# Delta-rule chunk tables: two stages of 256 tokens each against one stage of four units of 128 tokens

## The reference, cut to what matters

```
def step(S, inp):
    qt, kt, vt, at, bt = inp
    v_hat = einsum('bij,bi->bj', S, kt)
    err = vt - v_hat
    S = at * S + bt * (kt[:, :, None] * err[:, None, :])
    o = einsum('bij,bi->bj', S, qt)
    return (S, o)
_, O = lax.scan(step, S0, (Q, Kh, V, alpha, beta))
```

## Time and profile before

| | |
|---|---|
| time, median of 3 runs | 5346.77 us (5340.24 to 5348.16) |
| profiled execution, time | 5344.06 us |
| profiled execution, span | 5342.3 us |
| DVE busy | 4191.0 us (78%) |
| PE busy | 3706.5 us (69%) |
| ACT busy | 3022.2 us (57%) |
| POOL busy | 2649.8 us (50%) |

### The profile page before, as it was taken

How to read it: one execution, slowest core, us unless ns; L and a number is a source line. 1 busy time by engine, 2 the same in 40 slices (tenths; PEclk the granted TensorE clock), 3 DMA queues, 4 the chain that set the end, 5 groups by cost and what they waited for, 6 DMA issues and landing times. The chain is left out here.

```text
span 5342.3 us, 68134 instructions
## 1 busy us (share of the span) xinstructions
PE 3706.5 (69%) x15374; PEld 1423.1 (27%) x15374; DVE 4191.0 (78%) x7837; ACT 3022.2 (57%) x4244; POOL 2649.8 (50%) x2095
## 2 busy tenths in 40 slices
PE   7983000222222279698859999999999999999569
PEld 3431000122122234233213333333333333333123
DVE  5544956999999765426879999999999999999352
ACT  5575000222222155433728989898989898999432
POOL 1000644888888510120735666666666666666312
PEclk9997555666666699899979999999999999999789
DMA  1017054343344300001441111111111111110300
GB/s 43 8 42 125 8 91 88 80 88 85 77 87 88 85 25 10 10 0 74 159 137 34 35 35 34 34 35 35 35 31 33 25 34 35 35 35 5 103 10 32
DMA packets 143839, 275.50 MB, mean 52 GB/s; under 512 B 73808, under 2 KB 87504, under 8 KB 136336
## 3 DMA queue, kind: packets, MB, share of 16 engines
q1 hardware_dynamic: 142128, 263.57, 21.1%
q10 hardware_dynamic: 1440, 8.65, 0.5%
HBM read 178.65 MB, written 93.36 MB: 51 GB/s over the span
## 5 line engine op out<-in xcount | busy, mean ns | idle before, releaser
L1027 POOL TENSOR_TENSOR att_heads_rest<-att_heads_probs,att_heads_high 128x576 f16<-128x576 f32 x1024 | 1393.3, 1361 | 843.6 <-ACT att_heads_high L1114 836.9
L1144 DVE TENSOR_REDUCE att_heads_maxima<-att_heads_peek 128x1 f32<-128x512 f32 x2048 | 1311.3, 680 | 99.2 <-PE att_heads_peek L1040 71.1
L1112 ACT ACTIVATE att_heads_probs<-att_heads_scores 128x1024 f32<-128x1024 f32 x1024 | 1075.3, 1050 | 246.3 <-PE att_heads_scores L1058 237.9
L1058 PE MATMUL att_heads_scores<-att_heads_q,att_heads_k 128*128 128x512 f16 (+1 forms) x4096 | 1068.0, 383 | 34.2 <-issue 21.5
L1114 ACT ACTIVATE att_heads_high<-att_heads_scores 128x1024 f16<-128x1024 f32 x1024 | 1076.4, 1051 | 0.0
L1770 PE MATMUL delta_scan_sums<-delta_scan_o_halves,main_identity 128*128 128x256 f32 x768 | 245.4, 494 | 1111.2 <-POOL delta_scan_o_halves L1845 1111.2
L1164 DVE TENSOR_TENSOR att_heads_rest<-att_heads_probs,att_heads_high 128x448 f16<-128x448 f32 x1024 | 888.5, 868 | 64.8 <-POOL att_heads_rest L1027 53.3
L1040 PE MATMUL att_heads_peek<-att_heads_k,att_heads_q 112*128 112x512 f16 x2048 | 686.2, 396 | 89.1 <-DVE att_heads_maxima L1144 46.4
L1058 PEld LDWEIGHTS att_heads_scores<-att_heads_q,att_heads_k 128*128 128x128 f16 (+1 forms) x4096 | 394.6, 98 | 459.4 <-ACT att_heads_high L1114 39.8
L1770 PEld LDWEIGHTS delta_scan_sums<-delta_scan_o_halves,main_identity 128*128 128x128 f32 x768 | 194.4, 258 | 1162.6 <-POOL delta_scan_o_halves L1845 1124.4
L1074 PE MATMUL att_heads_out<-att_heads_high,att_heads_v_head 128*64 128x512 f16 x2048 | 419.3, 406 | 3.7 <-DVE att_heads_rest L1164 2.9
(11 more groups left out here) (243 smaller groups left out, 5180.4 us busy)
## 6 DMA issues: line engine op xcount, KB each, us to landing
delta_scan_record<-delta_record SPq DMA_DIRECT2D x64, 1026.0 KB, 10.9
att_heads_q<-att_hel SPq DMA_DIRECT2D x192, 128.0 KB, 3.1
att_heads_k<-att_hel SPq DMA_DIRECT2D x192, 128.0 KB, 3.2
delta_record<-delta_chunks_record SPq DMA_DIRECT2D x64, 256.5 KB, 4.8
att_hel<-att_hel_high SPq DMA_DIRECT2D x32, 512.0 KB, 4.4
att_hel<-att_hel_rest SPq DMA_DIRECT2D x32, 512.0 KB, 5.0
att_o<-att_heads_out_copy SPq DMA_DIRECT2D x256, 32.0 KB
att_out_parts<-att_o ACTq DMA_DIRECT2D x8, 1024.0 KB, 13.2
```

Of the source, the lines that this page charges most:

```text
L1027: nc.gpsimd.tensor_tensor(rest[:, step % 4, SPLIT:], probs[:, step % 4, SPLIT:], high[:, step % 4, SPLIT:], ALU.subtract).then_inc(rest_b_ ...
L1058: mm = nc.tensor.matmul(scores[:, step % 2, tokens(j)], k[0:rows, slot, number, tile * P:(tile + 1) * P], q[0:rows, slot, number, tokens(h ...
L1112: nc.scalar.activation(probs[:, step % 4], scores[:, step % 2], ACT.Exp, scale=LOGIT_SCALE).then_inc(probs_ready, 1)
L1144: nc.vector.tensor_reduce(maxima[:, m:m + 1], peek[:, m % 2], AX.X, ALU.max).then_inc(peek_read, 1)
```

## The change

The two calls become one, which goes over four units of 128 tokens of each part (16 chunks, two runs).

- Device memory: `delta_q` and `delta_k` become `(batch, part, unit, channel, 128)`; their stores in `delta_normalise` write pieces of 512 bytes. `delta_v` and the records keep their form.
- SP loads keys and queries of one unit, 8 + 8 transfers of 128 KB, into the single buffer `raw`, in the order (i, t); the load of unit u+1 is issued ahead of the stores of unit u, once both tiles of unit u have been turned. ACT issues the loads of the decays for all 512 tokens.
- ACT copies `raw` into `kq` in the order (t, i) (`turn`, one instruction for keys and one for queries, 2048 elements in a partition each, two buffers) and copies the turned keys into PSUM (`bank`, 2048 elements, one buffer).
- `gram` lies in PSUM. DVE's own products read the keys from PSUM (`k_bank`) and the other operand from SBUF. K_OUT reads `k_bank` too, 16 elements apart, and is made ahead of the solve.
- A row instruction now covers 16 chunks, so it has (t + w) x 256 elements. Of the 15 rows of a unit POOL multiplies 11 (44 x 256 elements in all, three slots) and DVE four: (0,3), (1,3), (0,5), (1,7), which is 20 x 256 elements.
- Each unit is finished and stored before the next is solved; the records of a unit wait for the stores of the unit before. SP, in order: load of unit u+1, stores of unit u.

The core of the diff:

```diff
-    RUNS = T // SPAN // PARTS // 2
-    N_CHUNKS = RUNS * CHUNKS
+    RUNS = UNIT // SPAN
+    N = UNIT // CHUNK
...
-        kq = s.sb("kq", [P, 2, RUNS, HD, SPAN])
+        raw = s.sb("raw", [P, 2, HD, UNIT])
+        kq = s.sb("kq", [P, 2, 2, UNIT, HD])
...
+        gram = s.ps("gram", [P, 2, N, C, C])
+        k_bank = s.ps("k_bank", [P, UNIT, HD])
...
-        own_rows = [row for row in rows if row[2] % 3 == 1 or row[1:] == (1, 3)]
+        rows = [(w, t) for t in range(C) for w in range(2) if w == 1 or t >= 1]
+        own_rows = [(0, 3), (1, 3), (0, 5), (1, 7)]
...
+        def row_product(engine, out, k, unit, w, t):
+            later = by_chunk(kq[:, unit % 2, w])[:, :, t].unsqueeze(2).broadcast_to([P, N, t + w, HD])
+            return engine.tensor_tensor(out[:, :, 0:t + w], by_chunk(k)[:, :, 0:t + w], later, ALU.mult)
...
+                load(0)
+                for unit in range(UNITS):
+                    if unit + 1 < UNITS:
+                        sp.wait_ge(turned, unit * 2 + 2)
+                        load(unit + 1)
+                    for run in range(RUNS):
...
+                        for b, part, at in places():
+                            sp.dma_start(dram["delta_record"][b, (part * UNITS + unit) * RUNS + run], record[at, run].rearrange("p m e -> p (m e)")
+                                         ).then_inc(stored[run], 16)
...
+                    for w, loaded in enumerate((k_loaded, q_loaded)):
+                        act.wait_ge(loaded, (unit + 1) * LOADS)
...
+                        nc.scalar.activation(kq[:, unit % 2, w].rearrange("p t i -> p i t"), raw[:, w], ACT.Copy).then_inc(turned, 1)
...
+                    nc.scalar.activation(k_bank[:], kq[:, unit % 2, 0], ACT.Copy).then_inc(banked, 1)
...
+                for unit in range(UNITS):
+                    row_sums(unit)
+                    k_out(unit)
+                    invert(unit)
+                    mixes(unit)
+                    if unit + 1 < UNITS:
+                        decays(unit + 1)
...
-    for part in range(2):
-        delta_chunks(nc, c, dram, f"{stage}_chunks{part}", part)
+    delta_chunks(nc, c, dram, f"{stage}_chunks")
```

More of the change, by code:

```diff
@@ L1529, in _, with delta_chunks @@
                     nc.vector.scalar_tensor_tensor(part, inv[:, k % 2], 1e6, part, ALU.min, ALU.mult).then_inc(unit_ready, 1)
-def delta_chunks(nc, c, dram, stage, number):
-    PARTS = P // BH
-    RUNS = T // SPAN // PARTS // 2
-    N_CHUNKS = RUNS * CHUNKS
+def delta_chunks(nc, c, dram, stage):
+    RUNS = UNIT // SPAN
+    N = UNIT // CHUNK
     C = CHUNK
     with Scope(nc, stage) as s:
-        kq = s.sb("kq", [P, 2, RUNS, HD, SPAN])
[L1546 to L1560, removed]
-        own_rows = [row for row in rows if row[2] % 3 == 1 or row[1:] == (1, 3)]
@@ L1566, in delta_chunks, with places @@
-        SLOTS = 4
+        POOLED, OWNED = len(pool_rows), len(own_rows)
+        LOADS = B * PARTS * 16
         SOLVED = 3 + 2 * (C - 1)
[L1569 to L1575, removed]
+        def places():
+            for b in range(B):
+                for part in range(PARTS):
+                    yield b, part, slice((b * PARTS + part) * HEADS, (b * PARTS + part + 1) * HEADS)
@@ L1589, in _ @@
-                for run in range(RUNS):
[L1590 to L1597, removed]
@@ L1601, in _ @@
+                for run in range(RUNS):
+                    sp.wait_ge(stored[run], UNITS * LOADS)
             @block.gpsimd
             def _(pool):
[L1603 to L1608, removed]
@@ L1618, in _, with turn @@
             @block.scalar
             def _(act):
[L1620 to L1626, removed]
+                def turn(unit):
+                    for w, loaded in enumerate((k_loaded, q_loaded)):
+                        act.wait_ge(loaded, (unit + 1) * LOADS)
+                        if unit >= 2 and w == 0:
+                            act.wait_ge(in_ready, (unit - 1) * RUNS * 2)
+                            act.wait_ge(own_ready, (unit - 1) * OWNED)
+                        nc.scalar.activation(kq[:, unit % 2, w].rearrange("p t i -> p i t"), raw[:, w], ACT.Copy).then_inc(turned, 1)
@@ new lines, in _ @@
+                turn(0)
+                bank(0)
+                for unit in range(UNITS):
+                    if unit + 1 < UNITS:
+                        turn(unit + 1)
+                        bank(unit + 1)
+                    act.wait_ge(solve_step, (unit + 1) * SOLVED)
+                    for run in range(RUNS):
+                        at = slice(run * CHUNKS, (run + 1) * CHUNKS)
+                        if unit >= 1:
+                            act.wait_ge(stored[run], unit * LOADS)
+                        nc.scalar.activation(record[:, run, :, SOLVE:SOLVE + C * C], solve[:, unit % 2, at].rearrange("p n t s -> p n (t s)"), ACT.Copy
+                                             ).then_inc(solve_copied, 1)
+                        nc.scalar.activation(record[:, run, :, DECAY], g[:, unit % 2, at, C, 0], ACT.Copy).then_inc(solve_copied, 1)
@@ L1638, in _ @@
[L1638 to L1652, removed]
-                        own += 1
@@ new lines, in mixes @@
+                def mixes(unit):
+                    for run in range(RUNS):
+                        at = slice(run * CHUNKS, (run + 1) * CHUNKS)
+                        nc.vector.tensor_tensor(record[:, run, :, MIX:MIX + C * C].rearrange("p m (t s) -> p m t s", s=C), gram[:, 1, at],
+                                                g[:, unit % 2, at, 1:, 1:], ALU.mult).then_inc(mix_ready, 1)
+                nc.vector.memset(g[:], 1.0).then_inc(zeroed, 1)
+                nc.vector.memset(solve[:], 0.0).then_inc(zeroed, 1)
```

185 lines of the change are left out of this document (125 added, 60 removed).

## The result

The changed kernel takes 5181.16 us in the median (5179.27 to 5184.21, 4 runs) where the kernel before took 5344.48 beside it: the ratio is 0.9695, with an interval of 0.9678 to 0.9712. That is 3.05% less. The forecast was 5151 us in a range of 5125 to 5200: the direction and the range hold, but the gain is 163 us and not the 195 that the forecast sums to (192.9 in the stage, 2.5 ahead of it), and the time lies outside the 5135 to 5175 that I gave the likeliest case. The table stage took what was forecast, within 3 us. What is missing was lost in a stage that the change does not touch.

The account below looks back on a forecast made before the run. No engine filled the table stages, so order counted: DMA bound loads and stores, DVE and POOL took turns. 71.3 + 202.4 + tail gave 227.1 us against 420.0; with 2.5 for the key store, 5151 us, range 5125 to 5200.

Parts of the forecast that it names:

- first unit: Table stage, from its start through unit one's loads, turn, products, solve and MIX: 71.3 us.
- last key store: Ahead of the table stage: storing keys in 512-byte pieces saves between nothing and 5.2 us; 2.5 us taken.
- Products and sums: Table stage, each unit: DVE's sums and its four own products take 25.1 us, never catching up with POOL.
- K_OUT: Table stage, each unit: two 1024-element products reading PSUM 16 elements apart, 1.97 us each, 4.0 us together.
- Solve and scaling: Table stage, each unit: half the elements in the same number of instructions, 11.1 us against 19.2 us before.
- POOL: Table stage, each unit: 11 products at 1.94 ns an element plus four 2.3 us records, 33 us, covered by DVE's 43.7.
- B: Rival, table stage: POOL stays slow and becomes the bound; 5170 us at 3.3 ns an element, 5240 at 4.7; chance 0.12.
- C: Rival, table stage: DVE's own products still take turns with POOL, 16 waits of 2.2 us, 5186 us; chance 0.05.
- E: Rival, table stage: POOL's cost per element grows with instruction length, eating the whole gain, up to 5353 us; chance 0.03.
- The joints: Table stage, units 2 and 3: load and turn stay hidden behind the unit before, with half a microsecond to spare.
- Rival A: Table stage: DMA sets the pace at two joints, 7 to 10 us each, 5168 to 5175 us; chance 0.14.
- The recurrence keeps its length: Sign for the stage behind the tables: its duration stays as before, so stage savings come off the time in full.

## Why the prediction was right, and where it was wrong

**The stage:** forecast 227.1 us, measured 224.6, by a mechanism that held, and with some luck: the terms were off by up to 3 us either way and offset each other. Term by term:

| term | forecast | measured |
|---|---|---|
| first unit | 71.3 | 74.0 |
| a further unit | 43.7 | 42.4 |
| tail | 24.7 | 23.4 |
| stage | 227.1 | 224.6 |
| last key store | -2.5 | -2.07 |

- *Products and sums*: DVE's 25.1 us were 25.3 (572.05 to 597.33 in the second unit), but with a wait of 1.5 us for POOL's last row inside. That DVE would not catch up with POOL was wrong by that much: POOL's last product was done after 23.3 us, not 22, and DVE's own work took 1.3 us less than forecast.
- *K_OUT* was mis-sized: I took 1.97 us from the solve's strided product, and it took 1.215 us, the price of the contiguous one, though it reads PSUM 16 elements apart. That is 1.5 us a unit too much, more than the 1.3 us that the unit was cheaper by; the solve took half a microsecond of it back.
- *Solve and scaling*: 11.6 us in the second unit against 11.1; in the first 16.1, where the TENSOR_SCALAR alone cost 5.43 us. This step failed in the first unit. I had asked of the decays whether two SBUF operands would make them wait for POOL, and not of an instruction with one. It explains the 2.7 us by which the first unit was longer, and more: the loads were 2 us faster than my sum.
- *POOL*: 2.2 ns an element, not 1.94, on the large products (3977 ns for 1792 against the 3.66 us forecast); the records 2.0 us, not 2.3. It stayed under DVE's time but for the 1.5 us above. Rivals B, C and E did not occur. (Two of their sums were off, without bearing on the forecast: B at 4.7 ns is 64 us a unit, not 66; E's line gives 8.0 ns at 1792 elements, not 7.8, and 5151 + 192 + 2.5 is 5346, not 5353.)
- *The last key store*: 2.5 us less forecast, 2.07 measured, within the scatter of the stage's start given above, so this term is not settled.
- *ACT*: turns 3685 ns against 3.6 us, the bank 1942 against 1.9.
- *The joints* had more room than the half microsecond: the queries of unit 2 were turned at 604.46 + 3.69 = 608.15, 38.1 us after the first unit's end, not 44.6. The 2.1 MB of loads were issued from 588.98 us on and had landed by 604.46, 15.5 us later, where I had 18.0 and some latency; from 589 to 604 us the engines moved 166 GB/s, with the last of the stores, against the 117 of loads alone. Rival A did not occur.

**The time:** the step that failed is "The recurrence keeps its length". It grew by 41.1 us, 39.1 of them the new waits, and this, less the 3.4 us won behind it, is the whole distance between what was won up to the recurrence (197.6) and what the span shows (159.9). I argued that nothing of the recurrence runs beside the tables and took from it that nothing of it changes; but an edit to one stage moves the code of every stage behind it. With the loop where it had been, the ratio of 0.9631 makes 5147 us of the 5344.48 before, 4 us under the forecast of 5151. So the stage was forecast to 3 us by the right mechanism, and the time missed by 30 us through a loss that none of my rivals had; the range held it because it had been made wide for other losses, which did not come.

The price of PSUM as a source stayed out of the sum rightly: DVE's product of 1024 elements with one operand in PSUM took 1216 ns, K_OUT from SBUF before 1.22 us. By the table of the Trainium skill ("VectorE: DVE Perf Modes", the section on the TRN2 errata) it would have been 4.4 us in all, an estimate; for these products the trace does not agree.

## What to carry to other kernels

After an edit, compare the length of the stages that were not edited, and look for an engine that waits on "issue" at a loop's first instruction, once a pass: a loop of 309 instructions gained or lost a fetch in each pass here by where it lay, and 49 idle instructions ahead of it settled that. Where DVE and GpSimd work side by side, give each DVE product one operand in PSUM, and where a short single-source DVE instruction on SBUF can wait for GpSimd, put it where GpSimd is idle (8 us here). Without contiguous inner operands the stage took 54 us more here, with its side effects, and a prefetch that hides a load behind a unit of compute 117.

## What the runs showed of the hardware that I had not expected

- The fetch of a loop: 2.6 us a pass for DVE, 36 to 41 us a kernel, by place in blocks of 128 instructions, and 78.0 us of waits in one place; 75 packets on an instruction queue come and go with it (253 against 178). Another 36 packets came with the change (178 against 142). The trace has 35 of them behind the recurrence (160 against 125 from `delta_out_inv` on), where the program did not become slower (3469 us against 3473); whose they are is open.
- A DVE TENSOR_SCALAR of 128 elements, SBUF to SBUF, took 277 ns with POOL stopped. With POOL busy it ended each time about 0.15 us behind the end of a POOL instruction: the first one after it had begun (0.92 us, three units), or only the last one before POOL fell idle, past four others (5.43 us, the first unit). Why it lets some go by is open. The Trainium skill ("SBUF — State Buffer", who interferes with whom) counts such an instruction among those that can take the pair of ports shared with GpSimd; that it can miss several turns is not stated there.
- A bank read 16 elements apart in PSUM cost DVE nothing in K_OUT: 1215 ns for 1024 elements, and 1215 again without the turn, where that operand is contiguous. A product whose operands both lay 128 elements apart, one in PSUM and one in SBUF, cost 1.76 ns an element.
